# A gated recurrent step in float32: how the four blocks of the reset gate are fed in three steps of four

## The reference

```python
def step(H, xs):
    xz, xr, xh = xs
    Z = jax.nn.sigmoid(xz + H @ Whz.T + bhz)
    R = jax.nn.sigmoid(xr + H @ Whr.T + bhr)
    H_tilda = jnp.tanh(xh + R * H @ Whh.T + bhh)
    H_new = Z * H + (1.0 - Z) * H_tilda
    Y = H_new @ Whq.T + bhq
    return (H_new, Y)
...
x = x + _L0_cond_ref(x, cond_1024, ...)
```

## Time and profile before

| | |
|---|---|
| median of three runs | 521.46 us (520.5 to 522.43) |
| the profiled execution's own time | 522.41 us |
| its span in the trace | 520.6 us |
| granted TensorE clock, mean | 0.997 of full |
| PE busy | 508.4 us, 98% |
| PEld busy | 491.0 us, 94% |
| ACT busy | 322.4 us, 62% |
| DVE busy | 306.6 us, 59% |

### The profile page before, as it was taken

How to read it: one execution, slowest core, us unless ns; L and a number is a source line. 1 busy time by engine, 2 the same in 40 slices (tenths; PEclk the granted TensorE clock), 3 DMA queues, 4 the chain that set the end, 5 groups by cost and what they waited for, 6 DMA issues and landing times.

```text
span 520.6 us, 96194 instructions
## 1 busy us (share of the span) xinstructions
PE 508.4 (98%) x44184; PEld 491.0 (94%) x44184; DVE 306.6 (59%) x1929; ACT 322.4 (62%) x1800; POOL 0.2 (0%) x4
## 2 busy tenths in 40 slices
PE   8499999999999999999999999999999999999997
PEld 7499999999999999999999999999999999999997
DVE  1256666666666666666566666666666666665664
ACT  2256666666666666666666666666666666666664
POOL 0000000000000000000000000000000000000000
PEclk9989999999999999999999999999999999999999
DMA  5011111111111111111211111111111111111111
GB/s 182 25 45 49 52 51 50 51 50 50 50 50 50 52 49 50 55 46 50 55 46 50 55 47 50 54 50 50 51 50 50 50 50 50 50 50 52 49 50 52
DMA packets 57737, 27.64 MB, mean 53 GB/s; under 512 B 6785, under 2 KB 56833, under 8 KB 57729
## 3 DMA queue, kind: packets, MB, share of 16 engines
q1 hardware_dynamic: 56880, 26.70, 18.3%
q10 hardware_dynamic: 848, 0.83, 0.5%
HBM read 18.98 MB, written 8.52 MB: 53 GB/s over the span
## 4 chain that ended last, share of the span: by engine, by line
PE 96%; issue 2%; DMA 1%; SPq 0%; DVE 0%; ACT 0%; ACTq 0%; DVEq 0%
PE r_ps L252 34%; PE c_ps L252 27%; PE z_ps L252 24%; PE y_ps L252 11%; DMA whq_sb<-in_whq_dram 1%; SPq L117 0%; SPq L119 0%; SPq L118 0%; SPq L115 0%; DVE h_sb L245 0%; DVE o_sb L219 0%; DVE rh_sb L232 0%; DVE u_sb L240 0%; ACT c_ps L193 0%; ACT y_ps L182 0%
## 5 line engine op out<-in xcount | busy, mean ns | idle before, releaser
L252 PE MATMUL c_ps<-xt_sb,wx_sb 128*32 128x64 f32 (+1 forms) x4104 | 174.4, 225 | 1.3 <-issue 1.3
L252 PE MATMUL z_ps<-xt_sb,wx_sb 128*32 128x64 f32 (+1 forms) x4104 | 168.1, 221 | 0.5 <-issue 0.5
L232 DVE TENSOR_TENSOR rh_sb<-y_ps,h_sb 128x32 f32<-128x32 f32 x512 | 89.7, 192 | 130.0 <-ACT y_ps L182 130.0
L182 ACT ACTIVATE y_ps<-r_ps 128x32 f32<-128x32 f32 x512 | 87.3, 182 | 98.4 <-PE r_ps L252 92.2
L252 PE MATMUL z_ps<-h_sb,whz_sb 128*32 128x32 f32 x8192 | 124.2, 198 | 2.2 <-issue 2.2
L252 PE MATMUL c_ps<-rh_sb,whh_sb 128*32 128x32 f32 x8192 | 123.0, 198 | 2.0 <-issue 1.9
L252 PE MATMUL y_ps<-whq_sb,h_sb 128*32 128x128 f32 x2064 | 112.2, 278 | 0.2 <-DVE h_sb L245 0.2
L252 PE MATMUL r_ps<-xt_sb,wx_sb 128*32 128x64 f32 (+1 forms) x4104 | 112.3, 220 | 0.0
L252 PEld LDWEIGHTS z_ps<-h_sb,whz_sb 128*32 128x32 f32 x8192 | 109.0, 111 | 2.4 <-issue 2.4
L252 PEld LDWEIGHTS c_ps<-rh_sb,whh_sb 128*32 128x32 f32 x8192 | 103.5, 110 | 2.3 <-issue 2.0
L252 PEld LDWEIGHTS z_ps<-xt_sb,wx_sb 128*32 128x32 f32 (+1 forms) x4104 | 104.6, 110 | 0.7 <-issue 0.7
(11 more groups left out here) (29 smaller groups left out, 438.1 us busy)
## 6 DMA issues: line engine op xcount, KB each, us to landing
xt_sb<-in_xt_dram SPq DMA_DIRECT2D x130, 64.0 KB, 1.7
xres_sb<-in_xr_dram SPq DMA_DIRECT2D x130, 64.0 KB, 1.8
out_dram<-o_sb SPq DMA_DIRECT2D x130, 64.0 KB, 1.6
wx_sb<-in_wx_dram SPq DMA_DIRECT2D x3, 256.0 KB, 3.2
whr_sb<-in_whr_dram ACTq DMA_DIRECT2D x1, 256.0 KB, 5.3
whz_sb<-in_whz_dram ACTq DMA_DIRECT2D x1, 256.0 KB, 5.5
whh_sb<-in_whh_dram ACTq DMA_DIRECT2D x1, 256.0 KB, 5.7
whq_sb<-in_whq_dram SPq DMA_DIRECT2D x1, 256.0 KB, 6.7
```

What stands on the lines that cost most here:

```text
L182: nc.scalar.activation(r_out[p][o], r_ps[:, o, here], ACT.Sigmoid).then_inc(s_r[o], 1)
L232: nc.vector.tensor_tensor(rh_sb[:, k], r_out[p][k], old[:, k], ALU.mult).then_inc(s_rh[k], 1)
L252: return nc.tensor.matmul(ps, weights, moving, start=start, stop=False, skip_group_check=True, **kw)
```

## The change

The fourth block joins the table for u = 1, 2 and 3, and its later part reads u in place of h; the wait for `s_h[0]` goes.

```diff
-AHEAD = [((1, 0),)] + [((0, 0), (1, 0), (1, 1))] * (SLOTS - 1)
+AHEAD = [((1, 0),)] + [((0, 0), (1, 0), (1, 1), (0, 1))] * (SLOTS - 1)
...
                         r_part(u, 1, 1, u_sb[:, 1])
-                        pe.wait_ge(s_h[0], done)
-                        r_part(u, 0, 1, old[:, 0]).then_inc(s_r_ps[1], 1)
+                        r_part(u, 0, 1, u_sb[:, 0]).then_inc(s_r_ps[1], 1)
```

## The result

The changed kernel takes 536.95 us (median of four runs, 536.61 to 539.06), the kernel before, run beside it, 521.94 us (520.5 to 522.97): **a ratio of 1.0294, 95% interval 1.0272 to 1.0316, 15 us slower**. Its profiled execution took 536.82 us, with a span of 534.9 us. The forecast was 533.4 us, in a range of 527.5 to 537.5: the right side and the right mechanism, with the price too small by a fifth.

The account below looks back on a forecast made before the run. TensorE's throughput was taken to bound u = 1, 2 and 3, the ACT and DVE chain only u = 0's entry. Added records' 12.0 us on 522.41 gave 534.4, less 0.95 to the median: 533.4 us, range 527.5 to 537.5.

Parts of the forecast that it names:

- TensorE's throughput bounds u = 1, 2 and 3: Claim that the array, not data, limits these steps: at u = 2 data were ready 0.11 us before it.
- Part 1: Eight more records over zh ahead of y in three bodies: 62 ns each time, 12.0 us in total.
- signs to look for: Expected profile if right: pass 7.95 us, zh's block 0.24 us, y to u 0.22, gap ahead of u = 0 near 0.18.
- upper bound: High end for the added records over zh ahead of y: 14.4 us.
- Part 2: In the reset gate's last block h becomes u, eight records for eight: no cost.
- part 3: The wait for h[0] goes at u = 1, 2, 3; met 0.04 us before it is asked: worth nothing.
- lower bound: At the seam from u's records to the update gate, up to 0.03 us a step regained: 5.8 us at most.
- half given back: Rival: added records cost 12.0 us, the seam without a wait returns 5.8: 528.6 or 527.7 us; chance 0.12.
- The hole at u = 0: Ahead of u = 0 the array idles 0.18 us, bound by the chain through ACT and DVE; it shifts with the pass.
- Part 4: Longer loop body, first pass: perhaps one more stop for instructions, 0 to 2.0 us once; taken as nothing.
- hidden: Rival: the ACT and DVE chain bounds u = 2 and 3 too, added records fill waiting: 515.7 or 521.5 us; chance 0.08.

Follow-up runs that it names:

- e1: Kernel before plus four unread matmuls over zh in the bodies of u = 0, 1 and 2, reset gate and wait kept: ratio 1.0302.
- e3: Kernel before with one split block less: at u = 1, 2, 3 block (1, 1) runs once, over h[1]: ratio 1.0032.
- e4: Changed kernel with the added block over zh issued behind y's four matmuls instead of ahead: ratio 1.0259 to the kernel before.
- e11: Kernel before plus two unread blocks over zh in each body of u = 0, 1 and 2: ratio 1.0546.
- e2: Kernel before with block (0, 1) at u = 1, 2, 3 reading u without waiting for h[0], no work added: ratio 1.0010.
- e7: Kernel before with all four blocks split at u = 0 too, 24 more records over zh in u = 3's body: ratio 1.0437.
- e6: Kernel before with block (0, 0) split at u = 0 too, four more matmuls over zh in u = 3's body: ratio 1.0109.
- e10: Kernel before plus four unread matmuls over zh in the body of u = 3 alone, ahead of y and the loop's jump: ratio 1.0085.
- e5: Kernel before with TensorE's loop alone unrolled over eight steps instead of four: 1419 us, ratio 2.716.

## Why the prediction was right, and where it wasn't

- **TensorE's throughput bounds u = 1, 2 and 3: shown for added work.** Unread work costs its full time (e1), and the data's lead over the array at u = 2 grew from 0.11 us to 0.21 (263.30 to 263.51). It doesn't hold for work taken away: in e3 the data bind at once.
- **Part 1, the added records: the mechanism right, the size too small.** Forecast 62 ns a block, 12.0 us; measured 15.0 us, 78 ns a block. Two things are missing. The rate of 7.8 ns a record, taken from twelve matmuls over zh, is a little low: a block costs 65 to 66 ns (e4, and the second block of e11), 192 x 3.6 ns = 0.7 us. And the price of the first block isn't only its rate: 0.035 us a pass, 2.2 us, are lost at the way into y and on to u, for which the sum had no term. The signs to look for had y to u unchanged at 0.22 and the block over zh at 0.24; they are 0.24 and 0.27 at u = 2. The part's upper bound, 14.4 us, was passed. That the total stayed in the range, by 0.5 us, is partly luck: the range had that room for a stop for instructions, not for this. The Trainium skill (TensorE: Matmul & The Clock Gate, Back-to-back issue gap) gives about 25 ns as an issue floor for small matmuls. The traces again contradict it as a floor from one record to the next: 32 records in 0.27 us are 8.4 ns each. If the records share the four strips evenly, one strip gets a record every 34 ns (an estimate, 4 x 8.4), and a floor of 25 ns within a strip would not be contradicted.
- **Part 2 and part 3, h for u and the missing wait: nothing, as forecast.** e2 has 1.001 (0.999 to 1.0029). The lower bound that I had given them, 5.8 us, is empty, and with it the rival "half given back". One reason that I gave was wrong: the 0.16 us between the two sigmoids are not ACT's own pace but the two blocks of TensorE between their signals (0.09 us with one block, in e7). The change keeps two blocks there, so nothing came of it.
- **The hole at u = 0: the conclusion right, the reason wrong.** I had written that the chain through ACT and DVE bounds the entry of u = 0 and that the array idles 0.18 us there; the step that failed took the profile's releaser, DVE, at its word. It is the jump. For this change it made no difference, as the hole moves with the work in either case. But what follows from my reason, that work ahead of the hole is free, is false by e6, e7 and e10.
- **Part 4, nothing for the longer body: about right.** PEld's waits labelled "issue" sum to 9.4 us before and 11.0 after. The first branch of TensorE's loop comes 1.3 us later in the changed kernel (27.1 for 25.8 us), but in the kernel before the pass behind it takes 9.2 us for 7.76, so in these two executions such stops nearly cancel.
- **The rival "hidden":** it would have shown as a smaller y to u; refuted there and by e1. What spoke for it was rightly read: at u = 2 and 3 the weight load over u does wait for its product. But the matmul behind it starts 0.10 us later, when the array gets to it.

## What to carry to other kernels

Splitting a sum so that a matmul needn't wait doubles that matmul's work. It pays only while the engine really waits there; a wait that is met 0.04 us early is worth nothing, and to see that, compare when the data are heard with when the queue gets there, and not whether a wait is written. A busy share doesn't tell where an engine is full: an unread copy of the work, put where the new work would stand, prices it directly. And where the profile names a releaser, see whether its data came one signal ahead of the engine's start (0.05 us here) or long before: in the second case something else held the engine.

## What the runs showed of the hardware that I had not expected

- A loop's jump on TensorE costs some 0.35 us from the last weight load to the first of the next pass, 344 ns of it from the start of a branch record of 208 ns; the matmuls in flight cover about half of it (0.18 us remain of the 0.40 from y to u, less the 0.22 that y takes elsewhere). Work ahead of it doesn't fill it: 0.09 us a pass for eight records (e10).
- A body of 344 matmuls (688 records of each kind) seems to be kept, one of 688 not: instructions by DMA went from 0.10 MB to 6.28 MB and the time from 522 to 1419 us (e5).
- Eight records of 32 columns cost 65 to 66 ns, but 78 where they lengthen a run from 24 to 32 ahead of matmuls with 128 columns.
